# Regrouping the second batch's normalisation and reordering four projection units in an attention kernel

## The chip, the cores and the metric

The kernel runs on one core of a Trainium2 chip. The metric is device time in microseconds (us) of one execution, 2652.79 in the median of three runs before the change. Five engines work side by side and meet at semaphores: TensorE (PE) multiplies, VectorE (DVE), ScalarE (ACT) and GpSimd (POOL) work on elements, and SyncE (SP) issues the transfers, all of which go through one queue in the order of issue.

## The reference

Two batches of 2048 tokens with 1024 features go through one block: x is normalised over its features, projected to q, k and v of 16 heads, attended causally, projected again, normalised and added to x; a gated expert layer follows, which the change doesn't touch.

```python
q = (x @ wq.T + bq).reshape(B, S, H, hd)      # k and v likewise, x normalised
scores = jnp.einsum('bqhd,bkhd->bhqk', q, k) * inv_sqrt_hd
scores = jnp.where(causal[None, None, :, :], -jnp.inf, scores)
probs = jax.nn.softmax(scores, axis=-1)
attn = jnp.einsum('bhqk,bkhd->bqhd', probs, v).reshape(B, S, D)
return attn @ wo.T + bo
```

## The kernel before

**Pairs and steps.** Two heads of one batch make a pair; there are 16 pairs, 0 to 7 for batch 0 and 8 to 15 for batch 1. A pair has 24 steps. Three steps make a round: one long row tile of queries in two chunks of keys (8 blocks of 128 keys, then 8 down to 1), and one short row tile (1 up to 8 blocks). Each engine runs its own list of instructions, written out step by step in a function `body(p, kind)`, and waits for the others through counters.

**What a step holds.** In step i of pair p TensorE makes the scores of step i + 3 (`scores`, line 371), then a part of a projection unit for pair p + 1, then multiplies the probabilities of step i with v (`times_v`, lines 395 to 397). For step i + 3, VectorE takes the row maximum of both heads (`row_max`, 511), ScalarE the exponential (686) and the high half (692), GpSimd the low half (784), and SyncE transposes the result (`transpose_probs`, 278) into a ring of four tiles, `pt`. For each transpose SyncE waits until TensorE has used the tile that stood there four heads ago; so the transposes for step i + 3 follow TensorE's step i + 1. In every third step VectorE also evacuates the outputs of the last round (532 to 550). TensorE's scores of a step wait for the exponential of the first head of the step before it.

**Projection units.** q, k and v of a pair come in four chunks of 512 tokens each, twelve units, two steps for each unit. Their order is written out in `UNITS`: "mid" for most pairs, "pre" in pair 6 and "turn" in pair 7, the last two being the same list. The weights of a pair are fetched into one raw buffer, `w_raw` (line 269), and split into two halves by ScalarE (668) and VectorE (487). `SPLITS` puts the split of q at step 1, and those of k and v at the step after the last unit of k and of v. SyncE fetches the next weights one step after a split, behind that step's transposes, and only when VectorE has finished with `w_raw`. The order of the fetches is k, v, q.

**The second batch.** The normalised tokens lie in `arena`. Those of batch 0 must stay until pair 7 is projected, which pair 6 does. So batch 1's 16 tiles of tokens are normalised on the side during pairs 0 to 6, each in three parts: `norm_stats` (load waited for, 462, and GpSimd's `norm_scale`), `norm_apply` (472, and ScalarE's `xn_high`, 661), and `xn_low` (477). A tile is then stored to `xn_scratch` (301) and the next loaded into `x_in`, both ahead of SyncE's transposes of the following step. The parts stand at `FREE_STEPS`, the steps 1, 4, 7 and so on to 22 of each pair, three steps apart. From step 8 of pair 6 to step 14 of pair 7 SyncE transposes the tiles from `xn_scratch` into `arena` (line 263), one at each second step, in the order of chunks 0, 1, 3, 2.

Of the kernel before, what the change touches and what calls it, by code (L numbers as in the profile page):

```python
# [50 lines left out]
for i in range(QT // 2):  # L51
# [13 lines left out]
UNITS = {"start": [(m, c) for c in range(4) for m in "kqv"],  # L65
         "mid": [("k", 0), ("k", 1), ("k", 2), ("k", 3), ("q", 3), ("q", 0), ("v", 0), ("v", 1), ("v", 2), ("v", 3),
                 ("q", 1), ("q", 2)],
         "turn": [("k", 0), ("q", 0), ("v", 0), ("k", 1), ("q", 1), ("v", 1), ("k", 3), ("q", 3), ("k", 2), ("v", 3),
                  ("v", 2), ("q", 2)],
         "last": []}  # L70
UNITS["pre"] = UNITS["turn"]
# [10 lines left out]

LN_TILES = S // P


FREE_STEPS = [(p, i) for p in range(PAIRS) for i in range(1, NSTEP, PER_ROUND)][1:]
NORM_STEPS = {tile: FREE_STEPS[3 * tile:3 * tile + 3] for tile in range(LN_TILES)}


def norm_tiles(p, i, part):  # L90
    return [tile for tile, at in NORM_STEPS.items() if at[part] == (p, i)]

TURN_CHUNKS = [0, 1, 3, 2]
TURN_TILES = [4 * c + i for c in TURN_CHUNKS for i in range(4)]
# [12 lines left out]
def attend_phase(nc, x, w_pairs, unit_in, mask_in, xn_scratch, o_scratch, arena, fin):  # L109
    with ExitStack() as ctx:  # L110
# [120 lines left out]
        def next_split(p, kind, i):  # L231

            m = SPLITS[kind].get(i)
            target = p + 1 if m == "q" else p + 2
            return (target, m) if m and target < PAIRS else None
# [20 lines left out]
        def _(sp):  # L256
            def load_x(tile, sem_, b, t):
                sp.dma_start(tile[:], x_view[b, t]).then_inc(sem_, 16)
# [32 lines left out]
            def body(p, kind):  # L291
                for i in range(NSTEP):
                    n = TURN_STEPS.get(kind, {}).get(i)
                    if n is not None:
                        tile = TURN_TILES[n]
                        sp.wait_ge(xn_stored, 16 * (tile + 1))
                        sp.wait_ge(unit_done, units_before(HALF_PAIRS - 1, [(m, tile // 4) for m in "qkv"]))
                        transpose_x(LN_TILES + n, tile, xn_scratch[tile])
                    for tile in norm_tiles(p, i - 1, 2):
                        sp.wait_ge(xn_lo_done, LN_TILES + tile + 1)  # L300
                        sp.dma_start(xn_scratch[tile], xn[:]).then_inc(xn_stored, 16)
                        if tile + 1 < LN_TILES:
                            load_x(x_in, x_loaded[P_RING], 1, tile + 1)
                    if p == 0 and i == 0:
                        load_x(x_in, x_loaded[P_RING], 1, 0)
                    step = step_of(p, i, kind)
                    if step:
                        transpose_probs(*step)
                    split = next_split(p, kind, i - 1)
                    if split:  # L310
                        target, m = split
                        after = {"q": (target + 1, "k"), "k": (target, "v"), "v": (target, "q")}[m]
                        if after[0] < PAIRS:
                            load_weight(*after)
                    if i == 14:
                        store_rows(p, 0)
                    if p > 0 and i == 2:
                        store_rows(p - 1, 1)
                    if kind == "last" and i == 0:
                        sp.wait_ge(unit_done, N_UNIT * PAIRS)  # L320
                        sp.wait_ge(s_done, NTASK * (PAIRS - 1))
                        sp.wait_ge(mix_set, 2)
                        for k in range(4):
                            sp.dma_start(wo_raw[k], fin["w_view"][k]).then_inc(wo_loaded[k], 16)
                        for tile, source in fin["loads"]:
                            sp.dma_start(tile, source).then_inc(fin_loaded, 16)
                    if kind == "last" and i >= 4 and i < KT:
                        sp.wait_ge(wo_lo_done, i - 3)
                        sp.dma_start(wo_raw[i % 4], fin["w_view"][i]).then_inc(wo_loaded[i % 4], 16)
                if kind == "last":  # L330
                    store_rows(p, 1)
# [120 lines left out]
        def _(dve):  # L452
# [141 lines left out]
            def body(p, kind):  # L594
                for i in range(NSTEP):
# [13 lines left out]
                        split_weight(*split)  # L609
                    if i % PER_ROUND == 0:  # L610
                        row_min(p, i // PER_ROUND)
                    for tile in norm_tiles(p, i, 0):
                        norm_stats(LN_TILES + tile, x_in, x_loaded[P_RING], tile)
                    for tile in norm_tiles(p, i, 1):
                        norm_apply(LN_TILES + tile, x_in)
                    for tile in norm_tiles(p, i, 2):
                        xn_low(LN_TILES + tile, x_in, xn)
                    if kind == "last":
                        if i == 0:
                            dve.wait_ge(unit_done, N_UNIT * PAIRS)  # L620
# [37 lines left out]
        def _(act):  # L658
# [59 lines left out]
            def body(p, kind):  # L718
                for i in range(NSTEP):
# [16 lines left out]
                        rows_high(2 * p + (0 if i == 13 else -1))  # L736
                    if kind == "last" and 2 <= i < 2 + KT:
                        wo_high(i - 2)
                    for tile in norm_tiles(p, i, 1):
                        if tile > 0:  # L740
                            act.wait_ge(xn_stored, 16 * tile)
                        xn_high(LN_TILES + tile, x_in, xn)
                if kind == "last":
                    rows_high(2 * p + 1)

# [23 lines left out]
        def _(pool):  # L769
# [39 lines left out]
            def body(p, kind):  # L809
                for i in range(NSTEP):  # L810
# [11 lines left out]
                        long_rows(*((p, i // PER_ROUND - 1) if i else (p - 1, N_ROUND - 1)))  # L822
                    if i == 13 or i == 1 and p > 0:
                        rows_low(2 * p + (0 if i == 13 else -1))
                    for tile in norm_tiles(p, i, 0):
                        norm_scale(LN_TILES + tile)
                if kind == "last":
                    long_rows(p, N_ROUND - 1)
                    rows_low(2 * p + 1)
# [608 lines left out]
```

## Time and profile before

| | us |
|---|---|
| runs | 2650.32, 2658.9, 2652.79 |
| median | 2652.79 |
| the profiled execution | 2650.32 |
| its span, first to last instruction | 2648.1 |
| TensorE busy | 2362.3 (89%) |
| GpSimd busy | 1813.9 (68%) |
| VectorE busy | 1752.9 (66%) |
| ScalarE busy | 1696.3 (64%) |

The span lies 2.2 us inside the execution's own time. The attention loop runs from about 150 to 2162 us; the rest is the first batch's preparation before it and the output projection with the expert layer behind it. A granted clock of 1.00 is TensorE's full 2.4 GHz.

### The profile page before, as it was taken

What the parts mean: (1) busy time and instruction counts of PE and PEld (TensorE: products, weight loads), DVE (VectorE), ACT (ScalarE), POOL (GpSimd) and SP (SyncE); (2) the same over time, 40 slices, a digit from 0 to 9 for tenths busy, and PEclk for the clock granted to TensorE, in tenths of its full rate; (3) what the DMA queues carried; (4) which work ended last, traced back from release to release, by engine and by line L of the source; (5) the groups of instructions that cost most, each with busy time, mean ns of one, the idle gap of its engine ahead of it and who ended that gap; (6) DMA issues with size and microseconds to landing.
All of it is one profiled execution on the core that took longest, in us unless ns stands there. A gap on an engine that the chain in (4) does not pass through costs nothing. (4 is left out here: it accounts for less than half of the span.)

```text
span 2648.1 us, 73681 instructions
## 1 busy us (share of the span) xinstructions
PE 2362.3 (89%) x29650; PEld 1508.7 (57%) x29650; DVE 1752.9 (66%) x3751; ACT 1696.3 (64%) x2425; POOL 1813.9 (68%) x1543
## 2 busy tenths in 40 slices
PE   3789999999999997899999999999997549999995
PEld 2457576666656655556675757676674325444543
DVE  6466767666766654566656666666656836888887
ACT  2277778777777765667777777777776533444444
POOL 2278788878878775778778778887887533555453
PEclk9999999999999998999999999999998669999997
DMA  8499999999999999999999999999999875777773
GB/s 200 102 165 192 193 191 204 181 188 182 199 180 186 183 179 183 187 175 177 175 164 178 169 174 168 184 164 173 171 167 190 162 142 111 155 156 152 148 157 95
DMA packets 1433793, 450.33 MB, mean 170 GB/s; under 512 B 1410256, under 2 KB 1411680, under 8 KB 1433456
## 3 DMA queue, kind: packets, MB, share of 16 engines
q1 hardware_dynamic: 1433456, 445.63, 92.9%
q8 instruction: 236, 3.87, 0.6%
q14 instruction: 101, 0.83, 0.1%
HBM read 68.01 MB, written 41.94 MB: 42 GB/s over the span
## 5 line engine op out<-in xcount | busy, mean ns | idle before, releaser
L784 POOL TENSOR_TENSOR hl<-probs,hl 128x1024 f16<-128x1024 f32 (+7 forms) x768 | 1227.7, 1609 | 449.9 <-ACT hl L692 447.4
L511 DVE TENSOR_REDUCE neg_max<-s_ps 128x1 f32<-128x1024 f32 (+7 forms) x768 | 696.3, 907 | 408.5 <-PE s_ps L377 342.7
L686 ACT ACTIVATE probs<-s_ps,exp_bias 128x1024 f32<-128x1024 f32 (+7 forms) x768 | 655.0, 853 | 475.7 <-DVE exp_bias L514 471.2
L692 ACT ACTIVATE hl<-probs 128x1024 f16<-128x1024 f32 (+7 forms) x768 | 620.5, 808 | 46.3 <-DMA pt<-hl 22.2
L395 PE MATMUL o_ps<-v,pt 128*128 128x65 f16 x4352 | 456.2, 195 | 88.4 <-DMA pt<-hl 71.1
L371 PE MATMUL s_ps<-nat 64*128 64x512 f16 (+3 forms) x3840 | 439.3, 358 | 70.6 <-ACT probs L686 68.7
L395 PEld LDWEIGHTS o_ps<-v,pt 128*128 128x128 f16 x4352 | 406.3, 98 | 136.1 <-DMA pt<-hl 65.6
L396 PE MATMUL o_ps<-v,pt 128*128 128x65 f16 x4352 | 456.1, 196 | 0.0
L397 PE MATMUL o_ps<-v,pt 128*128 128x65 f16 x4352 | 454.2, 194 | 0.0
L424 PE MATMUL u_ps<-arena,w 128*128 128x512 f16 x992 | 384.8, 388 | 55.2 <-DMA arena<-hl 41.2
L396 PEld LDWEIGHTS o_ps<-v,pt 128*128 128x128 f16 x4352 | 406.1, 98 | 27.1 <-issue 0.3
L397 PEld LDWEIGHTS o_ps<-v,pt 128*128 128x128 f16 x4352 | 406.7, 99 | 0.0
L425 PE MATMUL u_ps<-arena,w 128*128 128x512 f16 x992 | 381.5, 385 | 0.0
L426 PE MATMUL u_ps<-arena,w 128*128 128x512 f16 x992 | 381.0, 384 | 0.0
L420 PE MATMUL u_ps<-w,arena 128*128 128x128 f16 x1984 | 340.7, 220 | 1.8 <-DVE full L503 1.8
L421 PE MATMUL u_ps<-w,arena 128*128 128x128 f16 x1984 | 339.4, 220 | 0.0
L422 PE MATMUL u_ps<-w,arena 128*128 128x128 f16 x1984 | 339.3, 220 | 0.0
L371 PEld LDWEIGHTS s_ps<-nat 64*128 64x128 f16 x3840 | 162.5, 96 | 219.0 <-issue 91.2
L420 PEld LDWEIGHTS u_ps<-w,arena 128*128 128x128 f16 x1984 | 194.1, 98 | 28.8 <-issue 20.9
L424 PEld LDWEIGHTS u_ps<-arena,w 128*128 128x128 f16 x992 | 97.5, 98 | 197.4 <-issue 85.2
L1054 PE MATMUL proj_ps<-arena,ot 128*128 128x512 f16 x512 | 196.2, 383 | 14.1 <-DMA ot<-o_scratch 14.1
L1055 PE MATMUL proj_ps<-arena,ot 128*128 128x512 f16 x512 | 195.9, 383 | 0.0
(147 smaller groups left out, 3774.2 us busy)
## 6 DMA issues: line engine op xcount, KB each, us to landing
w_raw<-in_w_pairs SPq DMA_DIRECT2D x48, 576.0 KB, 4.8
o_scratch<-o_hl SPq DMA_DIRECT2D x128, 128.0 KB, 3.5
x_in_c<-in_x SPq DMA_DIRECT2D x32, 512.0 KB, 5.9
out<-result SPq DMA_DIRECT2D x32, 512.0 KB, 4.2
pt<-hl SPq DMA_TRANSPOSE x768, 4.5
probs<-in_x SPq DMA_DIRECT2D x16, 512.0 KB, 4.7
x_in<-in_x SPq DMA_DIRECT2D x16, 512.0 KB, 5.3
xn_scratch<-xn SPq DMA_DIRECT2D x16, 512.0 KB, 3.8
```

The costliest lines, as they stand in the source:

```text
L371: mm = nc.tensor.matmul(s_ps[(n + h) % S_RING][:, at:end], qk[HEADS[h], q, rows], qk[HEADS[h], k, keys], start=(q == q_lo), stop=(q == q_h ...
L395: nc.tensor.matmul(dst, lo, v_hi, start=(first and k == 0), stop=False)
L396: nc.tensor.matmul(dst, hi, v_lo, start=False, stop=False)
L397: mm = nc.tensor.matmul(dst, hi, v_hi, start=False, stop=(last and k == nb - 1))
L420: nc.tensor.matmul(dst, xt[:, 1, k, toks], hi[:, k, :], start=first, stop=False)
L424: nc.tensor.matmul(bank, lo[:, k, :], xt[:, 0, k, toks], start=first, stop=False)
L425: nc.tensor.matmul(bank, hi[:, k, :], xt[:, 1, k, toks], start=False, stop=False)
L426: mm = nc.tensor.matmul(bank, hi[:, k, :], xt[:, 0, k, toks], start=False, stop=last)
L511: nc.vector.tensor_reduce(neg_max[:, r, acc, h:h + 1], s_ps[n % S_RING][:, 0:nb * P], AX_X, ALU.max, negate=True).then_inc(max_done, 1)
L686: nc.scalar.activation(probs[n % P_RING][:, 0:nb * P], s_ps[n % S_RING][:, 0:nb * P], ACT.Exp, bias=exp_bias[:, r, acc, h:h + 1], scale=SO ...
L692: nc.scalar.activation(hl[n % HL_RING][:, 0:nb * P], probs[n % P_RING][:, 0:nb * P], ACT.Copy).then_inc(p_hi_done, 1)
L784: nc.gpsimd.tensor_tensor(hl[n % HL_RING][:, w:2 * w], probs[n % P_RING][:, 0:w], hi, ALU.subtract).then_inc(p_lo_done, 1)
```

## The change

The three parts of a tile's normalisation stand on three steps in a row, beginning at steps 5, 12 and 19 of pairs 0 to 4 and at step 5 of pair 5, which holds the sixteenth tile. SyncE loads a tile three steps before the first part, and stores it in the step of the third part; both stand behind that step's transposes. The transposes from `xn_scratch` wait for all sixteen stores in place of their own. In the list "turn" (and "pre") units seven to ten become q3, k3, v3, k2 in place of k3, q3, k2, v3.

```diff
-         "turn": [("k", 0), ("q", 0), ("v", 0), ("k", 1), ("q", 1), ("v", 1), ("k", 3), ("q", 3), ("k", 2), ("v", 3),
+         "turn": [("k", 0), ("q", 0), ("v", 0), ("k", 1), ("q", 1), ("v", 1), ("q", 3), ("k", 3), ("v", 3), ("k", 2),
                   ("v", 2), ("q", 2)],
...
-FREE_STEPS = [(p, i) for p in range(PAIRS) for i in range(1, NSTEP, PER_ROUND)][1:]
-NORM_STEPS = {tile: FREE_STEPS[3 * tile:3 * tile + 3] for tile in range(LN_TILES)}
...
+NORM_STEPS = [{3 * p + i: 5 + 7 * i for i in range(3)} for p in range(5)] + [{15: 5}] + [{}] * (PAIRS - 6)
...
-                        sp.wait_ge(xn_stored, 16 * (tile + 1))
+                        sp.wait_ge(xn_stored, 16 * LN_TILES)
...
-                    for tile in norm_tiles(p, i - 1, 2):
-                        sp.wait_ge(xn_lo_done, LN_TILES + tile + 1)
-                        sp.dma_start(xn_scratch[tile], xn[:]).then_inc(xn_stored, 16)
-                        if tile + 1 < LN_TILES:
-                            load_x(x_in, x_loaded[P_RING], 1, tile + 1)
-                    if p == 0 and i == 0:
-                        load_x(x_in, x_loaded[P_RING], 1, 0)
                     step = step_of(p, i, kind)
                     if step:
                         transpose_probs(*step)
+                    for tile, at in NORM_STEPS[p].items():
+                        if i == at - 3:
+                            if tile >= 1:
+                                sp.wait_ge(xn_lo_done, LN_TILES + tile)
+                            load_x(x_in, x_loaded[P_RING], 1, tile)
+                        if i == at + 2:
+                            sp.wait_ge(xn_lo_done, LN_TILES + tile + 1)
+                            sp.dma_start(xn_scratch[tile], xn[:]).then_inc(xn_stored, 16)
...
-                    for tile in norm_tiles(p, i, 0):
-                        norm_stats(LN_TILES + tile, x_in, x_loaded[P_RING], tile)
-                    for tile in norm_tiles(p, i, 1):
-                        norm_apply(LN_TILES + tile, x_in)
-                    for tile in norm_tiles(p, i, 2):
-                        xn_low(LN_TILES + tile, x_in, xn)
+                    for tile, at in NORM_STEPS[p].items():
+                        if i == at:
+                            norm_stats(LN_TILES + tile, x_in, x_loaded[P_RING], tile)
+                        if i == at + 1:
+                            norm_apply(LN_TILES + tile, x_in)
+                        if i == at + 2:
+                            xn_low(LN_TILES + tile, x_in, xn)
```

ScalarE's `xn_high` moves to step `at + 1` and GpSimd's `norm_scale` to step `at` in the same way.

## Rows read from the trace of the kernel before

**Rows 1.** Busy time by stretch: length, busy us (instructions), granted clock, DMA share, GB/s.

```profile
263.00:890.20 627.20, 593.76 (x8481) 398.52 (x8480) 434.27 (x876) 466.12 (x656) 508.84 (x379) 0.99 1.07 189
890.20:1169.60 279.40, 247.36 (x3392) 161.60 (x3392) 147.73 (x324) 182.61 (x260) 191.88 (x141) 0.95 1.03 181
1169.60:1776.80 607.20, 587.34 (x8483) 395.33 (x8484) 380.49 (x812) 454.47 (x649) 483.04 (x351) 1.00 1.02 173
```

**Rows 2.** Timeline, VectorE's first instruction after pairs 6 and 12: start, us, instruction, wait.

```profile
1026.44 0.43 DVE L532 TENSOR_TENSOR o_part<-o_ps,factor 128x260 f32<-128x260 f32 x1 [1.46 <-PE o_ps L397]
...
1776.87 0.43 DVE L532 TENSOR_TENSOR o_part<-o_ps,factor 128x260 f32<-128x260 f32 x1 [0.70 <-PE o_ps L397]
```

**Rows 3.** TensorE's waits, 150 to 890 us: total, times, longest.

```profile
PE o_ps L395 <- DMA pt<-hl: 23.1, 24, 3.7
PE s_ps L371 <- ACT probs L686: 10.6, 14, 1.4
```

**Rows 4.** Timeline of TensorE at the turn, pair 6 and pair 7.

```profile
905.31 0.61 PE L424 MATMUL u_ps<-arena,w 128*128 128x512 f16 x1 [2.65 <-DVE w L487]
...
1046.65 0.61 PE L424 MATMUL u_ps<-arena,w 128*128 128x512 f16 x1 [7.00 <-DVE w L487]
...
1129.60 0.58 PE L424 MATMUL u_ps<-arena,w 128*128 128x512 f16 x1 [3.86 <-DMA arena<-xn_scratch]
```

**Rows 5.** Busy time by stretch, after two of these waits.

```profile
1046.60:1052.00 5.40, 5.35 (x17) 2.05 (x18) 0.00 (x0) 2.06 (x5) 4.48 (x4) 0.50 0.86 169
1129.60:1136.00 6.40, 6.40 (x42) 2.83 (x44) 0.00 (x0) 0.00 (x0) 1.30 (x2) 0.67 0.91 177
```

**Rows 6.** Timeline of SyncE's issues at the end of pair 6.

```profile
1013.33 0.57 SPq L269 DMA_DIRECT2D w_raw<-in_w_pairs  x1
...
1017.94 9.62 SPq L278 DMA_TRANSPOSE pt<-hl  x4
...
1038.89 0.57 SPq L269 DMA_DIRECT2D w_raw<-in_w_pairs  x1
```

**Rows 7.** Timeline of ScalarE in the same stretch.

```profile
1020.67 1.04 ACT L668 ACTIVATE w<-w_raw 128x1024 f16<-128x1024 f32 x1
...
1021.99 0.35 ACT L686 ACTIVATE probs<-s_ps,exp_bias 128x128 f32<-128x128 f32 x1
...
1044.21 1.06 ACT L668 ACTIVATE w<-w_raw 128x1024 f16<-128x1024 f32 x1 [4.85 <-DMA w_raw<-in_w_pairs]
```

**Rows 8.** The page's DMA issues: count, KB each, median us from issue to landing.

```profile
w_raw<-in_w_pairs SPq DMA_DIRECT2D x48, 576.0 KB, 4.8
```

**Rows 9.** Timeline at the end of pair 7, SyncE (to 1170 us) and TensorE.

```profile
1159.81 10.85 SPq L278 DMA_TRANSPOSE pt<-hl  x4
...
1170.04 1.47 PE L371 MATMUL s_ps<-nat 64*128 64x512 f16 x12 [0.42 <-ACT probs L686]
```

**Rows 10.** The tile x_in: durations ns min/median/max, first and last start; waits.

```profile
L472 DVE TENSOR_SCALAR x_in<-x_in,moments_a,rstd_a x16: 805/1288/2671, 182.5 to 885.5; 128x1024 f32<-128x1024 f32 x16
...
L477 DVE SCALAR_TENSOR_TENSOR xn<-x_in,xn x16: 1214/1548/2629, 196.9 to 901.2; 128x1024 f16<-128x1024 f32 x16
...
  DMA x_in<-in_x: 25.1, 14
```

**Rows 11.** Timeline of TensorE: step 6 of pairs 3 and 10, step 23 of pair 10.

```profile
548.60 0.24 PE L395 MATMUL o_ps<-v,pt 128*128 128x65 f16 x1 [3.74 <-DMA pt<-hl]
...
1449.12 0.20 PE L395 MATMUL o_ps<-v,pt 128*128 128x65 f16 x1 [1.46 <-DMA pt<-hl]
...
1530.72 0.34 PE L371 MATMUL s_ps<-nat 64*128 64x128 f16 x6 [1.40 <-ACT probs L686]
```

**Rows 12.** Timeline of VectorE, step 21 of pair 10.

```profile
1524.86 3.18 DVE L487 SCALAR_TENSOR_TENSOR w<-w_raw,w 128x1024 f16<-128x1024 f32 x1
```

**Rows 13.** Timeline of SyncE's issues, step 2 of pair 3.

```profile
530.20 0.77 SPq L301 DMA_DIRECT2D xn_scratch<-xn  x1
531.02 0.42 SPq L258 DMA_DIRECT2D x_in<-in_x  x1
```

More of the change, by code:

```diff
@@ L83 @@
 LN_TILES = S // P
-FREE_STEPS = [(p, i) for p in range(PAIRS) for i in range(1, NSTEP, PER_ROUND)][1:]
-NORM_STEPS = {tile: FREE_STEPS[3 * tile:3 * tile + 3] for tile in range(LN_TILES)}
-def norm_tiles(p, i, part):
-    return [tile for tile, at in NORM_STEPS.items() if at[part] == (p, i)]
+NORM_STEPS = [{3 * p + i: 5 + 7 * i for i in range(3)} for p in range(5)] + [{15: 5}] + [{}] * (PAIRS - 6)
 TURN_CHUNKS = [0, 1, 3, 2]
@@ L738, in body @@
                         wo_high(i - 2)
[L739 to L742, printed above, removed]
+                    for tile, at in NORM_STEPS[p].items():
+                        if i == at + 1:
+                            if tile > 0:
+                                act.wait_ge(xn_stored, 16 * tile)
+                            xn_high(LN_TILES + tile, x_in, xn)
                 if kind == "last":
@@ L824, in body @@
                         rows_low(2 * p + (0 if i == 13 else -1))
-                    for tile in norm_tiles(p, i, 0):
-                        norm_scale(LN_TILES + tile)
+                    for tile, at in NORM_STEPS[p].items():
+                        if i == at:
+                            norm_scale(LN_TILES + tile)
                 if kind == "last":
```

## The prediction

> **What bounds the kernel now.** First the busy table by stretch: the attention loop runs its 16 head pairs at a nearly even pace, and in pairs 8 to 12 (1169.6 to 1776.8 us) TensorE is busy 587.3 of 607.2 us at the full clock [rows 1]. TensorE is the bound there; every other engine has room. So a microsecond of other work costs nothing until it keeps TensorE waiting. The five pairs 1 to 5, which do the same attention work and carry most of the second batch's normalisation besides, take 627.2 us [rows 1]; their ends are read from VectorE's first instruction of the next pair [rows 2]. Normalisation therefore costs 20.0 us in five pairs, or 4.0 us a pair. Pairs 6 and 7, where the second batch's tokens replace the first's, take 279.4 us where two of the quiet pairs take 2 x 607.2 / 5 = 242.9 [rows 1]: 36.5 us too many. The change touches both places and nothing else, so at most some 56 us stand to be moved.
>
> Next the waits of TensorE. In the normalising stretch the longest in total are for transposed probabilities (23.1 us) and for ScalarE's exponentials (10.6) [rows 3]. At the turn, three single waits matter: 2.65 us and 7.00 us for the weights of q, and 3.86 us for the last token tiles [rows 4]. A wait costs more than itself, because the clock falls: after the wait that ends at 1046.65 TensorE works from 1046.6 to 1052.0 at a granted clock of 0.50, that is 1.2 GHz, so 5.4 us ran at half speed and 2.7 us were lost on top of the 7.00 [rows 4, 5].
>
> **The order of the units.** In pair 7 the old order asks for token chunk 2 with its ninth unit, at step 16, two steps after the last tile of it was sent for; the new order asks with the tenth, at step 18. The 3.86 us wait goes [rows 4], and with it its low clock: the 6.4 us of work behind it have a mean grant of 0.67, so 6.4 x 0.33 = 2.1 us were lost [rows 5]. Gain: 5.9 us, to rounding. One step of cover (5 us) would have been enough; two are given.
>
> The same edit has a second effect, which the list doesn't show. The last k unit moves from ninth to tenth, so the split of k's weights moves from step 18 to 20, while the last v unit stays eleventh and its split at 22. There is one raw buffer for the three weights: SyncE may fetch v's only after k's split, so the fetch moves from its step 19 to its step 21, and ScalarE wants it at 22. SyncE issues it behind the two transposes of step i + 3, and these wait for TensorE to have used the tiles of step i + 1; SyncE is thus two or three steps behind. Before, the fetch left at 1013.33 and ScalarE used it at 1020.67 without a wait [rows 6, 7]. Two steps later in the same queue is the point after the four transposes that end at 1017.94 + 9.62 = 1027.56 [rows 6]. A fetch takes about 4.7 us to land (4.8 in the median of all 48; the one issued at 1038.89 let ScalarE go at 1044.21, 5.3 us on) [rows 6, 7, 8]. So ScalarE stands from 1020.7 to 1032.3, then splits (1.04). Queued behind it is the exponential that before ran at 1021.99, and for that one waits TensorE's first scores of pair 7, at 1026.4 [rows 2, 7]. It comes at 1032.3 + 1.0 + 0.4 + about 0.2 for the hand-over = 1033.9. TensorE waits 7.4 us, and 2.7 of clock as after the other 7 us wait: 10.1.
>
> Part comes back. The present 7.00 us wait for q has the same pattern (fetch behind late transposes), and with TensorE held up, SyncE's backlog is gone. I let it shrink to the 2.65 us of pair 6, which gives 4.4 and some 1.0 of clock: 5.4. Net in pair 6 and early pair 7: +4.7.
>
> At the end of pair 7 the same: the four transposes that begin at 1159.81 end at 1170.66, landing 1175.3, exponential through at 1176.8; TensorE wanted it at 1170.04 - 0.42 = 1169.6 [rows 9]. 7.2 us, less the 0.42 already waited there, plus 2.7: +9.5. No wait for q follows there, since the next pair wants q only with its fifth unit. Off this I take 3 us over both turns, an estimate, for transposes that catch up while TensorE stands. Turn: 4.7 + 9.5 - 5.9 - 3.0 = +5.3. Bounds: if each fetch lands as TensorE asks, -5.9; if nothing is given back and nothing caught up, 10.1 + 9.5 - 5.9 = +13.7.
>
> The Trainium skill (DMA: Bandwidth & Descriptors, Specifications, and Latency and other measured facts) gives 358 GB/s from HBM and about 2 us of fixed cost. As an estimate, that makes 3.6 us for a fetch of 576 KB, and with it the two waits would be 1.1 us shorter each, the turn +3.1. The landings of this trace, 1 us longer, speak against it.
>
> **The normalisation.** The sixteen tiles keep all their instructions. Before, the three parts of a tile lie three steps apart, always on a step without the evacuation of outputs; now they lie on three steps in a row, from steps 5, 12 and 19, so that one part always meets the evacuation, and SyncE loads three steps ahead and stores two steps after. The distance from a load to its use stays as it was: before, a load stood ahead of the transposes of step i and was used at i + 2; now it stands behind those of at - 3 and is used at `at`. So VectorE's waits for x_in, 25.1 us over 14 of the tiles, remain [rows 10]. For each of pairs 0 to 4:
> - SyncE's step 2 already has four stores of outputs, and TensorE waited 1.46 us at step 6 of pair 10 [rows 11]. Now a load stands before them: 0.43 us to issue, and 512 KB, which at the stretch's 189 GB/s is 2.8 us of the queue [rows 1]. 0.4 to 3.2; I take 0.8, since part meets slack.
> - Step 14 likewise with a store of xn. 0 to 3.2; I take 0.8.
> - Step 21 is VectorE's fullest: evacuation, two maxima of 1024, a unit, and v's split, which takes 3.18 us and ends at 1528.04; TensorE then waits 1.40 us, until 1530.72, for the exponential behind the next maximum [rows 11, 12]. xn's low part, 1.2 to 2.6 us [rows 10], now stands ahead of that maximum. +1.6 (0 where the split is short, up to 2.6).
> - The rest (x_in late, rstd waited for, the applying step on the evacuating step 6): 0.5 a tile, 1.5 (0 to 3).
> - The low clock behind the longer of these waits: 0.7 (0 to 1.7 each in two places).
>
> That is 5.4 a pair, 27 in five pairs, and 1 for the sixteenth tile, 28, against 19.6 now (the 20.0, less 0.4 by which pair 0 is quick and pair 6's part counts). +8. Its ends: small items alone, 1.0 a pair, is 5 + 1 - 19.6 = -14; all items high, about 9 a pair, is +26.
>
> The Trainium skill (SBUF — State Buffer, SBUF: two separate sides) says that VectorE and GpSimd lock one port pair for a whole instruction, the later one waiting. The applying instruction, 0.81 us alone and up to 2.67 here, fits [rows 10]. By that rule alone its cost is the same at whatever step it stands, which is for the first rival below.
>
> **Sum.** 2650.3 (the profiled execution; span 2648.1) + 5.3 + 8.0 = 2663.6. The three runs have their median 2.5 us above that execution; I put the forecast between, at 2665.
>
> **The rivals.**
> - Normalisation costs what it did, turn as worked out: 2655.6. For it: mean instruction times don't depend on the step, and VectorE has 30% idle time [rows 1]. 0.24.
> - Faster: today's cost is SyncE's store and load side by side ahead of the transposes (0.77 and 0.42 us, followed by a 3.74 us wait of TensorE [rows 11, 13]); apart, each stays within SyncE's slack, a pair costs 1.0 us, and -13.6 + 5.3 gives 2642.0. It decides from 1.1 us a pair down. Against: both now fall beside the output stores. 0.15.
> - VectorE falls behind over its three steps in a row, the wait at step 23 grows to over 3 us in every pair and the clock falls each time: 9 a pair, 2682. 0.13.
> - The fetch of v is hidden after all, or lands just in time (turn -5.9), normalisation +8: 2652. Against: it is queued behind the very transposes timed above. 0.06.
> - The forecast itself: 0.42.
>
> **Numbers.** Within 0.3% (8 us) is what a measurement of this kernel can't tell from no change: the first and fourth rival, 0.30. Faster is the second, 0.15. Slower is the forecast and the third, 0.55. The range leaves out half of the second's case and half of the third's, so 2642 to 2682; with both signs in it, the forecast's own is 2658 to 2674.
>
> **What would show it.** Right: TensorE's waits for ScalarE's exponentials of some 7 us at the starts of pairs 7 and 8, ScalarE standing there for w_raw; no wait for xn_scratch; the 7 us wait for q's weights under 3; waits at steps 6, 18 and 23 of pairs 0 to 4 longer, pairs 1 to 5 over 630 us. Wrong: pairs 1 to 5 below 620 us, or v's fetch landed before ScalarE asks.

## The result, and the profile after

| | before | after |
|---|---|---|
| median, us (five runs each) | 2653.22 | 2678.71 |
| range, us | 2650.32 to 2658.9 | 2669.97 to 2682.93 |
| the profiled execution | 2650.32 | 2673.91 |
| its span | 2648.1 | 2671.7 |

The changed kernel is slower: its time is 1.0095 of the time before, with a 95% interval of 1.0077 to 1.0113. The forecast had 2665 us: the direction is right and the time falls within the range, but the loss is 25.5 us by the medians and 23.6 by the profiled executions, where the forecast's sum had 13.3. The time lies outside the forecast's own 2658 to 2674.

First, where the time went. The busy table by stretch, cut at the same places as [rows 1] (columns as there):

```profile
269.30:912.00 642.70, 601.60 (x8483) 400.64 (x8484) 427.39 (x875) 465.48 (x657) 501.17 (x377) 0.98 1.03 183
912.00:1186.00 274.00, 242.49 (x3393) 159.95 (x3392) 144.98 (x322) 180.50 (x253) 191.80 (x141) 0.96 1.03 180
1186.00:1800.70 614.70, 588.31 (x8484) 394.71 (x8484) 379.00 (x812) 455.83 (x651) 483.20 (x351) 0.99 1.01 172
```

Pairs 1 to 5 take 642.7 us, 15.5 more than in [rows 1]; pairs 6 and 7 take 5.4 less, and pairs 8 to 12 take 7.5 more, since one new wait stands just behind the cut, in step 0 of pair 8. Pair 0 and the preparation account for another 6.3 (pair 1 begins at 269.3, not 263.0). Normalisation is thus the large item: the end of pair 5 comes at 912.0 and not 890.2, 21.8 us late, out of 23.6. The turn is the small one: +4.0 us over pairs 6 to 8, from 912.0 to 1316.8 (404.8) against 890.2 to 1291.0 (400.8). What follows is 2.2 us shorter.

The waits of TensorE in the normalising stretch, over the 150 to 890 us of [rows 3] (total us, times, longest; up to the end of pair 5 at 912.0 the exponentials' total is 11.7):

```profile
PE o_ps L388 <- DMA pt<-hl: 31.2, 19, 4.0
PE s_ps L364 <- ACT probs L680: 10.3, 12, 2.4
PE o_ps L388 <- issue: 3.7, 4, 2.1
```

Waits for the transposed probabilities, which hang on SyncE's queue, grew from 23.1 to 31.2 us. Those for exponentials nearly kept their total, but the longest is 2.4 us instead of 1.4. TensorE's timeline has it in step 23 of pair 2, and waits for transposes in steps 6 and 13 of pair 3, the first of which answers to the 3.74 us of [rows 11]:

```profile
522.64 0.51 PE L364 MATMUL s_ps<-nat 64*128 64x128 f16 x6 [2.44 <-ACT probs L680]
...
567.33 0.24 PE L388 MATMUL o_ps<-v,pt 128*128 128x65 f16 x1 [3.76 <-DMA pt<-hl]
...
603.39 0.20 PE L388 MATMUL o_ps<-v,pt 128*128 128x65 f16 x1 [0.78 <-DMA pt<-hl]
```

The turn, in the same view. The first and the third row answer to the first two of [rows 4], the last to TensorE's of [rows 9]:

```profile
927.22 0.39 PE L417 MATMUL u_ps<-arena,w 128*128 128x512 f16 x1 [3.62 <-DVE w L480]
...
1048.65 0.61 PE L364 MATMUL s_ps<-nat 64*128 64x512 f16 x2 [7.94 <-ACT probs L680]
...
1065.33 0.61 PE L417 MATMUL u_ps<-arena,w 128*128 128x512 f16 x1 [3.63 <-DVE w L480]
...
1159.33 0.23 PE L388 MATMUL o_ps<-v,pt 128*128 128x65 f16 x1 [3.24 <-DMA pt<-hl]
...
1193.60 1.01 PE L364 MATMUL s_ps<-nat 64*128 64x512 f16 x3 [7.56 <-ACT probs L680]
```

The waits of 7.94 and 7.56 us at the starts of pairs 7 and 8 are the forecast's late fetches of v. The wait of 7.00 us for q's weights is 3.63. The 3.86 us wait for xn_scratch is gone; two steps later stands one of 3.24 us for a transpose, which the forecast did not have. The timelines of SyncE and of ScalarE show the reason of the wait of 7.94 us:

```profile
1041.99 1.23 SPq L261 DMA_DIRECT2D w_raw<-in_w_pairs  x1
```

```profile
1046.83 1.06 ACT L662 ACTIVATE w<-w_raw 128x1024 f16<-128x1024 f32 x1 [9.19 <-DMA w_raw<-in_w_pairs]
1048.16 0.35 ACT L680 ACTIVATE probs<-s_ps,exp_bias 128x128 f32<-128x128 f32 x1
```

The fetch is issued at 1041.99. ScalarE stands 9.19 us for it, splits the weights, and only then does the exponential that TensorE wants; at 1048.65 TensorE resumes. Before, the same fetch left 13.1 us ahead of the end of pair 6 [rows 2, 6]; now it leaves 1.3 us behind it (pair 6 ends at 1040.7). The changed wait for all sixteen stores to `xn_scratch` plays no part: the last of them is issued at 841.7 us and the first transpose from there at 964.3.

**The excess table.** Two kernels that differ in order can't be compared by one wait. For the comparisons below I took the length of every step (the end of the last product with v of a step, less that of the step before) and subtracted the shortest length that the profiles show for a step of that number, in whatever pair (most pairs have the list "mid"). What remains is that step's excess. Its zero is thus a convention; only differences between rows are read. "6-7" and so on are steps of pairs 0 to 5, added up; (7,0) is step 0 of pair 7. One execution each, us:

```
       end of    pairs 0-5                           pairs 6-8
       pair 5    total   6-7    13   18-19   23      total  (7,0) (8,0) (7,2) (7,16) (7,18-19)
before  890.2     47.7  12.2   0.2    7.6   6.0       50.9    0.8   0.5   9.7    5.9    0.0
after   912.0     68.5  25.2   4.7   11.7  14.4       54.9    9.4   9.9   5.3    0.0    6.3
e8      910.7     67.4  23.4   4.9   12.8  14.3       57.5    9.7   9.0   5.4    0.0    3.8
e1      891.1     49.2  13.3   0.4    7.2   6.3       61.7   10.3  10.0   5.4    0.0    5.6
e2      911.9     69.7  25.1   4.8   16.0  13.2       50.1    0.8   0.7   7.6    5.8    0.0
e3      895.0     51.8  15.7   0.8    7.2   6.0       63.4   10.6  10.0   5.4    6.0    0.0
e4      906.6     63.7  31.0   4.9   13.7   1.5       60.2   11.0   9.8   5.2    0.0    4.7
e5      893.2     51.7  13.2   6.1    1.3   3.6       59.2   10.8   9.0   5.1    0.0    2.9
e9      895.2     53.3  23.4   4.3    1.0   5.6       63.1   10.9  10.3   5.1    0.0    6.1
e10     899.1     56.2  14.2   0.0   11.1  20.5       56.7    9.7   9.3   5.4    0.0    3.2
e6      894.5     51.9   8.5   1.6    8.0   5.7       53.5    0.0   0.7   6.1    0.0    3.6
e7      901.2     57.5  13.0   2.4    4.5   9.4       53.0    0.9   0.7   5.2    6.4    0.0
e11     884.4     42.6   1.1   0.4    1.0   2.9       52.9    0.8   0.2   7.8    6.6    0.0
e12     892.9     49.4  10.6   5.4    0.0   5.1       52.7    9.4  10.2   5.3    0.0    0.9
e13     879.7     37.7   0.6   1.0    0.1   8.8       51.2    0.1   0.6   4.4    0.0    0.9
e14     883.4     40.6   2.1   0.0    0.9   9.4       55.8    1.0   0.6   4.3    6.2    0.0
```

Its grain: e8 is the changed kernel once more, and e1, e3, e6 and e7 have the normalisation of before. Their pairs 0 to 5 lie 1.5, 4.1, 4.2 and 9.8 us above the first profile of before. So differences under about 4 us in one total say nothing, one of 10 can come from a single execution, and the first profile of before was a quick one: the mean of the five is 51.6.

### The profile page after: what moved, and what is told of

Same layout as the page of the kernel before. It is cut to its first block and busy times, and to the rows that moved or that the text cites. A ratio compares the mean times of both kernels' runs of the same rounds, so it can differ in the third digit from the quotient of the medians.

```text
span 2671.7 us, 73681 instructions
## 1 busy us (share of the span) xinstructions
PE 2364.8 (89%) x29650; PEld 1506.2 (56%) x29650; DVE 1747.5 (65%) x3751; ACT 1696.2 (63%) x2425; POOL 1808.3 (68%) x1543
```

## The experiments

### Which half costs: the order, the regrouping, the split (e1 to e3)

`e1_units_only` is the kernel before with only the new list of units:

```diff
- ("v", 1), ("k", 3), ("q", 3), ("k", 2), ("v", 3),
+ ("v", 1), ("q", 3), ("k", 3), ("v", 3), ("k", 2),
```

> The kernel before with the new order of the units alone. Theory A (as the changed kernel's trace reads): TensorE waits some 7.9 us for an exponential at the start of pair 7 and some 7.6 us at the start of pair 8, each with about 2.7 us of low clock behind it; the 3.86 us wait for the last token tiles is gone and the 7.0 us wait for q's weights shrinks to 3.6. Sum +4 us, 2654 in the profiled execution, ratio 1.001 to 1.003. Theory B (the two new waits carry the whole slowdown and the regrouping is harmless): +20 us or more, ratio from 1.007.

`e2_regroup_only` is the changed kernel with that line set back.

> The changed kernel with the old order of the units. Theory A: the regrouped normalisation costs 20 us more than the old one in pairs 0 to 5, and the turn reads as before (waits 7.0 and 3.9 us): ratio 1.006 to 1.009, about 2672. Theory B (regrouping harmless): ratio within 1.002 of 1.

`e3_k_split_late` keeps the old order and moves only the split of k's weights to step 20:

```diff
+SPLITS["pre"] = SPLITS["turn"] = {1: "q", 20: "k", 22: "v"}
```

> The kernel before with its old order of units, but the split of k's weights in pairs 6 and 7 moved from step 18 to step 20, and nothing else. It isolates the fetch. Theory A (v's fetch is late because it waits for k's split): the two waits of 7 to 8 us at the starts of pairs 7 and 8 appear without the new order; the 3.86 us wait stays; the q wait shrinks. +10 us (8 to 13), ratio 1.003 to 1.005. Theory B (the new waits come from the order of the units itself, e.g. k2 needed sooner than it is ready): no such waits, ratio 1.000.

Each ratio here and below is to runs of the kernel before on the same chip, whose median is given. Against 2661.48: e1 2670.14, ratio 1.0039 (1.0023 to 1.0056); e2 2674.43, 1.0057 (1.0040 to 1.0074); e3 2676.58, 1.0055 (1.0035 to 1.0076). Both halves cost, and their ratios multiply to 1.0096, that of the whole change. e1 and e3 cost more than their expectations allowed (1.003 and 1.005 at most), e2 a shade less (1.006 at least). In the excess table e1 has the turn's new waits and none of the normalisation's, e2 the reverse: the halves are independent. e3 shows the cause of the turn's: with the old order and its wait at step 16, one changed split step brings both late fetches and 12.5 us over pairs 6 to 8, in TensorE's timeline:

```profile
1036.11 2.75 PE L372 MATMUL s_ps<-nat 64*128 64x512 f16 x12 [8.07 <-ACT probs L687]
...
1183.53 2.74 PE L372 MATMUL s_ps<-nat 64*128 64x512 f16 x12 [7.73 <-ACT probs L687]
```

### What in the regrouping costs (e4, e5, e9)

`e4_low_late` moves only the last part of each pair's third tile, `xn_low` and its store, from step 21 to 22:

```diff
+low_at = lambda at: at + 3 if at == 19 else at + 2
...
-                        if i == at + 2:
+                        if i == low_at(at):
```

> The changed kernel with the low part (and the store) of the third tile of each pair moved from step 21 to step 22, behind the row maximum for which TensorE waits at step 23. Theory A (the low part stands ahead of that maximum): TensorE's waits at step 23 of pairs 0, 2 and 4 fall from 2.2 to 2.4 us to 1.4 or less, the clock behind them stays full, and pairs 0 to 5 lose about 8 us: 2666 in the profiled execution against 2674. Theory B (step 23 waits because of VectorE's whole load in three steps, not the order): step 23 unchanged.

`e5_io_apart` moves two of SyncE's transfers out of the steps that hold the output stores: the load of the first tile from step 2 to 1, the store of the second from step 14 to 15.

```diff
-                        if i == at - 3:
+                        if i == (1 if at == 5 else at - 3):
...
-                        if i == at + 2:
+                        if i == (15 if at == 12 else at + 2):
```

> The changed kernel with only SyncE's places changed: the load of the first tile at step 1 in place of 2, the store of the second at step 15 in place of 14, so that neither is issued in the step of the output stores. Theory A (they delay the transposes that queue behind the output stores): the waits at step 6 of pairs 1 to 5 fall by 1.5 to 2 us each and those at 18 by about 1, with their low clock; 12 us less in pairs 0 to 5, 2662. Theory B (what counts is the extra traffic and issue anywhere in the queue): the waits move a step with them, and pairs 0 to 5 change by less than 3 us.

Against 2659.16: e4 2676.68, ratio 1.0075 (1.0062 to 1.0087); e5 2669.60, 1.0033 (1.0016 to 1.0050). e4 removed its wait (step 23: 14.4 to 1.5 us), yet pairs 0 to 5 fell only 4.8, where about 8 were expected: steps 6 and 7 rose from 25.2 to 31.0. Whether that is the gain given back or a difference between executions, one profile can't tell, and the time's interval overlaps that of the changed kernel. e5 took 16.8 us off pairs 0 to 5 (68.5 to 51.7): 12.0 at steps 6 and 7, 10.4 at 18 and 19, 10.8 at 23, and 14.3 came back at steps 1, 2 and 20. TensorE's waits over pairs 0 to 5 in e5:

```profile
PE o_ps L388 <- DMA pt<-hl: 30.4, 28, 3.3
PE s_ps L364 <- ACT probs L680: 5.1, 6, 2.4
```

The total is as large as after the change, but in 28 pieces, the longest 3.3 us. Step 23 shows something more. VectorE's low part of a third tile takes 3.08 us or 1.21, and in these two kernels TensorE waits more than 0.4 us behind it only where it takes 3.08. VectorE in pair 4, after and then in e5:

```profile
775.00 3.09 DVE L470 SCALAR_TENSOR_TENSOR xn<-x_in,xn 128x1024 f16<-128x1024 f32 x1
```

```profile
759.88 1.21 DVE L470 SCALAR_TENSOR_TENSOR xn<-x_in,xn 128x1024 f16<-128x1024 f32 x1
```

TensorE's wait behind these, in the same order:

```profile
780.71 0.34 PE L364 MATMUL s_ps<-nat 64*128 64x128 f16 x6 [2.22 <-ACT probs L680]
```

```profile
763.71 0.34 PE L364 MATMUL s_ps<-nat 64*128 64x128 f16 x6 [0.29 <-ACT probs L680]
```

After the change, the third tile's low part is the long one in pairs 0, 2 and 4, whose step 23 has 4.0 to 4.2 us of excess each; in e5 it is long in pair 2 alone, which has 2.5 of e5's 3.6. So e5's gain at step 23 is a shift of VectorE against its neighbours, brought about by the moved transfers but not asked for.

`e9_low_io` has both edits.

> The changed kernel with both repairs of the regrouping: the third low part and its store one step later, and SyncE's load and store out of the steps of the output stores. Theory A (both act, each on its own waits): pairs 0 to 5 some 20 us shorter than in the changed kernel, near the kernel before; ratio 1.002 to 1.004, what is left being the turn's 8 us. Theory B (the two share a cause): no better than the moved transfers alone, 17 us.

Against 2653.12: 2665.52, 1.0040 (1.0027 to 1.0054), pairs 0 to 5 at 53.3. The two repairs don't add up. With SyncE's transfers apart, moving the low part brought nothing more.

### Issue time or traffic (e10), and the changed kernel again (e8)

`e10_load_small` is the changed kernel with 15 of the 16 loads cut to an eighth. SyncE issues the same instructions; the second batch is computed from other data.

```diff
-                            load_x(x_in, x_loaded[P_RING], 1, tile)
+                            if tile == 0:
+                                load_x(x_in, x_loaded[P_RING], 1, tile)
+                            else:
+                                sp.dma_start(x_in[:, 0:P], x_view[1, tile][:, 0:P]).then_inc(x_loaded[P_RING], 16)
```

> The changed kernel with the loads of the second batch's tiles 1 to 15 cut to 128 of 1024 columns (so the second batch is computed from other data; all instructions stay). It tells the 512 KB of a load from its place in SyncE's list. Theory A (traffic): the waits at step 6 fall from some 3 us to 1.5 in the mean, those at step 13 go, 10 us less. Theory B (SyncE's issue time of 0.5 to 1 us a transfer): both stay within 0.5 us.

> The changed kernel once more, beside the others of this set: how well its waits repeat. Pairs 0 to 5 within 4 us of the first profile, the waits at the starts of pairs 7 and 8 again 7.5 to 8 us, ratio 1.007 to 1.010.

e10: 2665.25, 1.0051 (1.0034 to 1.0069); e8: 2685.15, 1.0107 (1.0081 to 1.0134). With small loads steps 6 and 7 fall from 25.2 to 14.2 and step 13 from 4.7 to 0.0, both the steps that a load stands ahead of (steps 2 and 9). So it is the 512 KB in the queue that delay the transposes behind them, not the 0.4 to 1.1 us that a load takes to issue. Steps 18 and 19, behind a store, stay (11.7 to 11.1), as they should. Step 23 rose to 20.5, with waits for exponentials up to 4.5 us:

```profile
PE o_ps L391 <- DMA pt<-hl: 20.8, 13, 3.7
PE s_ps L367 <- ACT probs L683: 19.1, 16, 4.5
```

The low part of the third tile is the long one in four pairs here (1 to 4), where it was in three. The longest wait, though, stands in pair 0, whose low part took 1.34 us: there the two VectorE instructions of v's split ahead of it are the long ones, 2.04 and 3.16 us where the changed kernel's pair 0 has 0.22 and 1.22. VectorE and TensorE in e10:

```profile
256.51 3.16 DVE L483 SCALAR_TENSOR_TENSOR w<-w_raw,w 128x1024 f16<-128x1024 f32 x1
```

```profile
263.62 0.34 PE L367 MATMUL s_ps<-nat 64*128 64x128 f16 x6 [4.48 <-ACT probs L683]
```

So what moves step 23 here is how long VectorE's instructions in step 21 take, the low part or the split; none of these waits is for a transfer.

### The output stores (e11, e12)

In both kernels SyncE issues four output stores one after another in step 2 and again in step 14. `e11_stores_spread` is the kernel before with one in each of steps 2 to 5 and 14 to 17:

```diff
-                    if i == 14:
-                        store_rows(p, 0)
-                    if p > 0 and i == 2:
-                        store_rows(p - 1, 1)
+                    if 14 <= i < 18:
+                        store_rows(p, 0, [i - 14])
+                    if p > 0 and 2 <= i < 6:
+                        store_rows(p - 1, 1, [i - 2])
...
```

`store_rows` now takes the numbers of the stores that it is to issue.

> The kernel before with the four output stores of steps 2 and 14 issued one in each of steps 2 to 5 and 14 to 17. If TensorE's waits at steps 6 and 18, which also pairs without normalisation show, come from SyncE issuing four stores (2.6 to 2.9 us) ahead of the transposes, they fall to under 0.5 us in all pairs but the last: 2 us and 1 us with their low clock, 16 times, 20 to 40 us less, ratio 0.985 to 0.993, faster than both kernels. If they come from the traffic alone they spread and the ratio stays above 0.997.

`e12_spread_changed` is the same edit on the changed kernel.

> The changed kernel with the output stores spread over steps 2 to 5 and 14 to 17. Theory A (the regrouping costs what it does at steps 6 and 18 because its load and store meet the bunched output stores): the regrouping's extra 17 us over the old one shrink to under 8 in pairs 0 to 5, and this kernel is 30 us or more faster than the changed one, ratio 0.997 to 1.001 to the kernel before. Theory B (its transfers are late anywhere, the two costs add): 20 us faster than the changed one, and 25 us slower than the spread stores in the kernel before, ratio 1.002.

e11: 2628.73, 0.9912 (0.9894 to 0.9931) of 2653.12. e12: 2641.89, 0.9956 (0.9934 to 0.9979) of 2655.90. TensorE's waits over pairs 0 to 5, of e11 and then of e12:

```profile
PE o_ps L395 <- DMA pt<-hl: 24.0, 30, 1.7
PE s_ps L371 <- ACT probs L686: 9.4, 13, 1.5
```

```profile
PE o_ps L388 <- DMA pt<-hl: 33.3, 31, 3.2
PE s_ps L364 <- ACT probs L680: 4.9, 4, 1.9
```

In e11 the total of the waits for transposes is as large as before, but the longest is 1.7 us and not 3.7. Steps 6 and 7 fall from 12.2 to 1.1. Only 5.8 of the profile's 18.7 us come before the end of pair 5, and 13.3 in pairs 9 to 14 (724.5 us, then 711.2), which hold no normalisation: the bunched stores cost there too. What regrouping adds in pairs 0 to 5, 20.8 us with the stores bunched (68.5 less 47.7), is 6.8 with them spread (49.4 less 42.6). By means over all profiles with the same normalisation steps and the same stores it is 16.9 (68.5 less 51.6) and 9.1 (49.4 less 40.3, of e11, e13 and e14). So by the two ways of counting a little under a half or two thirds of its cost is the meeting with the bunched stores. The rest stays behind the loads: steps 6 and 7 are 9.5 us longer in e12 than in e11, step 13 is 5.0. Steps 1 and 20 are 11.8 longer, which no run explains, and other steps give most of all this back.

### Where step 16's gain goes (e6, e7, e13, e14)

In `e6_spare_new` every second weight from v of pair 8 on goes into a second raw buffer (x_in, by then unused, made wider); the fetch runs two weights ahead, so no split waits for it. It stands on the kernel before with the new list; `e7_spare_old` is the same with the old one.

```diff
+        def raw_of(at):
+            if at >= SPARE and (at - SPARE) % 2 == 0:
+                return x_wide, w_loaded2, (at - SPARE) // 2 + 1
+            return w_raw, w_loaded, at if at < SPARE else SPARE - 1 + (at - SPARE + 1) // 2
...
-                    sp.wait_ge(w_lo_done, weight_at(p, m) - 1)
+                    sp.wait_ge(w_lo_done, at - (1 if at < SPARE else 2))
```

> The kernel before with the new order of units, and from v of pair 8 on every second weight fetched into the idle x_in buffer (512 bytes a partition wider), so that a fetch no longer waits for the split just before it. Theory A (the fetch behind the last split is the whole of the two 7.5 us waits and of the q wait): no wait for exponentials above 2 us at the starts of pairs 7 and 8, q's wait at step 2 of pair 7 falls from 7.0 (before) and 3.6 (new order) to 2.7. Against the new order alone 15 to 20 us less, against the kernel before -5 to -9, ratio 0.997 to 0.998, if the 3.86 us saved at step 16 are not given back at step 18. Theory B: they are given back there (3.1 us wait for transposed probabilities, as in the new order alone), then -2 to -5.

> The same spare buffer with the old order of units. It tells the order's own worth once the fetch is out of the way. Theory A (the new order saves 5.9 us): this is 5 to 6 us slower than the spare buffer with the new order, with a 3.9 us wait at step 16 of pair 7. Theory B (the saving is given back at step 18): the two are within 2 us in pairs 6 to 8.

Against 2659.16: e6 2663.34, 1.0028 (1.0011 to 1.0046); e7 2661.73, 1.0018 (1.0003 to 1.0033). Neither is faster than the kernel before, where e6 was expected at 0.997 to 0.998. The spare buffer takes both late fetches away from the new order: (7,0) and (8,0) are 0.0 and 0.7, 19.6 us less than in e1. But pairs 6 to 8 are only 8.2 us shorter than in e1 (53.5 against 61.7). A part of the rest stands one step on, at (7,1), which the table doesn't show: its excess is 5.5 us in e6 and 0.0 in e1, with TensorE's wait for a transpose. TensorE in e6:

```profile
1044.40 0.19 PE L409 MATMUL o_ps<-v,pt 128*128 128x65 f16 x1 [3.02 <-DMA pt<-hl]
```

Between e6 and e7 the new order gains nothing. Both stretches of pairs 6 to 8, in the busy tables of e6 and of e7, are 403.5 and 403.0 us long. The 6.4 us at step 16 of e7 are in e6 3.6 at steps 18 and 19, 4.3 more at (7,1), and smaller items of both signs.

`e13_spread_spare_new` and `e14_spread_spare_old` are these two with the output stores spread as well.

> The kernel before with spread output stores, the spare weight buffer and the new order of units. Theory A (with SyncE in time, the 3.86 us saved at step 16 of pair 7 are no longer given back at step 18): 5 to 6 us less than with the old order, and q's wait falls from 6.2 to 2.6 us; pairs 6 to 8 about 12 us shorter than with spread stores alone: 2617, ratio 0.986. Theory B (given back wherever it stands): no better than spread stores alone but for q's wait, 2624.

> The same with the old order of units. Theory A: 5 to 6 us slower than with the new order, the 3.9 us wait for the last token tiles standing. Theory B: within 2 us of it.

Against 2655.90: e13 2623.77, 0.9875 (0.9847 to 0.9903); e14 2631.87, 0.9897 (0.9874 to 0.9919). The busy table over pairs 6 to 8, of e13 and then of e14:

```profile
879.70:1280.80 401.10, 364.09 (x5091) 241.53 (x5092) 228.31 (x487) 273.76 (x391) 290.75 (x212) 0.97 1.05 181
```

```profile
883.40:1289.20 405.80, 367.64 (x5092) 242.58 (x5092) 228.95 (x487) 273.83 (x391) 291.36 (x212) 0.96 1.04 179
```

With the stores of step 14 out of the way steps 18 and 19 cost 0.9 us, and the new order is worth 4.7 us here: the 6.2 of step 16 less small items. So what took the gain back at steps 18 and 19 was SyncE, still behind from the four stores of step 14, and not the order itself. The two intervals overlap (0.9847 to 0.9903, 0.9874 to 0.9919); that the order gains rests on this stretch of one profile each. The expectation that pairs 6 to 8 would be about 12 us shorter than with spread stores alone was missed: they are 1.7 shorter (51.2 against e11's 52.9), with 3.8 us of excess at (7,1). Most of e13's gain is e11's, and the intervals of these two overlap as well. By its median e13 is the best version: 1.25% under the kernel before and, by the two ratios (0.9875 / 1.0095 = 0.978), 2.2% under the changed one. It has the old normalisation steps, spread stores, the spare buffer and the new order.

## Why the prediction was right in direction and wrong in size

The step that failed is the price of the load that moved to step 2, 0.8 us a pair where 2.6 were measured, and beside it the load at step 9, which was not priced at all; both are in the part on the normalisation below.

**v's late fetch: right.** The forecast had waits of 7.4 and 7.2 us; they are 7.94 and 7.56, with 9.4 and 9.9 us of excess at (7,0) and (8,0), where it had 10.1 and 9.5. e3 makes them with the split alone, e6 takes them away with a buffer alone, though less than half of the time comes back with them.

**The wait for q: about right.** 7.00 us became 3.63 and not 2.65; "under 3" was missed. Its step, (7,2), gave back 4.4 us where 5.4 were forecast.

**Step 16: the step was right and its end was missed.** The 3.86 us wait and its clock are gone, as forecast, 5.9 us. But the prediction let that gain reach the end; 6.3 us came back at steps 18 and 19 (3.8 in e8, 5.6 in e1), except where the output stores were spread. The question of what is late next was put to the fetches and not to this gain. The 3.0 us taken off for transposes that catch up have a counterpart: the table's five columns at the turn add up to 14.0 us more than before and the total of pairs 6 to 8 to 4.0, so the other steps are 10.0 shorter; in e8, e1 and e3 they are 4.4, 3.6 and 2.6 shorter. The clearest of them is step 23 of pair 6, 4.5 us of excess before and 1.8 to 2.0 in these four; whether transposes that catch up are the cause no run shows. In sum the turn was forecast at +5.3. In the profiles of kernels with the new order, one raw buffer and bunched stores pairs 6 to 8 are 4.0, 6.6, 10.8, 9.3, 8.3, 12.2 and 5.8 us longer than before (after, e8, e1, e4, e5, e9, e10): 8.1 in the mean, within the given bounds of -5.9 and +13.7. That the first profile of after has 4.0, near the forecast, is in part luck.

**The normalisation: the failed step.** Forecast +8, measured +20.8 against the first profile of before and about +17 against the mean of those with unchanged normalisation. The upper end, "all items high, about 9 a pair", was added up wrongly: the bullets' own ends make 15.4 a pair, so it was no bound. By its bullets:
- Step 21, sized 1.6 a pair, 8 in five: step 23's excess rose by 8.4. Right in sum, but not as 1.6 in each pair: it is some 4 us, clock included, in the three pairs in which the low part takes 3.09 us, 0.4 in pairs 1 and 3, and 1.5 in pair 5, which has no third tile.
- Step 2's load, sized 0.8 a pair from a range of 0.4 to 3.2: steps 6 and 7 rose by 13.0, or 2.6 a pair. This is the failing term. "Part meets slack" was wrong: there was no slack, since four output stores are issued right behind the load, ahead of the transposes (SyncE's timeline, step 2 of pair 3, of after):

```profile
552.18 1.06 SPq L250 DMA_DIRECT2D x_in<-in_x  x1
553.30 0.42 SPq L261 DMA_DIRECT2D w_raw<-in_w_pairs  x1
553.76 2.91 SPq L280 DMA_DIRECT2D o_scratch<-o_hl  x4
556.78 14.18 SPq L270 DMA_TRANSPOSE pt<-hl  x6
```

  The end that the bullet worked out from the bytes of the load, 2.8 us, was the one to take; it was nearest to the row that it quoted beside it, the 3.74 us wait behind a store and a load [rows 11, 13].
- The load of step 9 was not priced at all; step 13 rose by 4.5, 0.9 a pair. This and the 1.8 us a pair missing at step 2 are 13.5 us in five pairs; the whole gap is 20.8 - 8 = 12.8.
- The load of step 16 was not priced either, and here nothing was lost: step 20, behind it, has 1.1 us of excess in six pairs, 2.2 before and 1.4 in e10, whose load there is an eighth. The same 512 KB thus cost 2.6, 0.9 or nothing by their place in the queue.
- Step 14's store, sized 0.8: steps 18 and 19 rose by 4.1, 0.8 a pair. Right.
- What went away was not seen. Steps 3, 4, 9, 14 and 15, where TensorE before stood for exponentials (up to 1.3 us at step 9) and transposes, fell from 12.6 us of excess to 1.8. The four rises above add up to 30.0; this and small changes elsewhere make it 20.8. Which of the moved parts had caused those waits no run tells.
- "VectorE's waits for x_in remain" was wrong, in the change's favour: 25.1 us over 14 tiles are 4.9 over 4. A load lands 4.6 us after its issue in the median (5.3 before), and VectorE is ready for the tile 5.2 us after the issue, not 3.4. The tile's rows, after:

```profile
L465 DVE TENSOR_SCALAR x_in<-x_in,moments_a,rstd_a x16: 803/806/1398, 179.1 to 822.2; 128x1024 f32<-128x1024 f32 x16
...
L470 DVE SCALAR_TENSOR_TENSOR xn<-x_in,xn x16: 1208/1923/3093, 183.5 to 832.8; 128x1024 f16<-128x1024 f32 x16
...
  POOL rstd_a L773: 9.1, 5
  DMA x_in<-in_x: 4.9, 4
```

  What it bought can't be told from the waits that went away at steps 3 to 15.

**The rivals.** That normalisation costs what it did fell with e2 (1.0040 to 1.0074). The faster one, store and load apart, fell too: they were parted from each other, but put beside four output stores, which cost more (e5 moves two of them off and the excess drops by 16.8 us). Its place, SyncE's queue, was where the change is decided, with the other sign. And VectorE's three steps in a row made no wait of over 3 us at step 23 in the changed kernel: 2.44 us was the longest, and three pairs of five have one of over 2.2. The fourth rival, v's fetch hidden after all, fell with the two waits of over 7 us. That rival's time, 2682, came nearer than the forecast's 2665, but its mechanism gave 8.4 us of the 20.8. With e10's 4.48 us one such wait exists in the record, in one pair.

**The applying instruction** was forecast to cost the same at any step by the rule of the Trainium skill (SBUF — State Buffer, SBUF: two separate sides): VectorE, where an instruction has two inputs in SBUF or runs in a mode with two ports, and GpSimd, where it reads SBUF, share one port pair and exclude each other for a whole instruction. Here its median fell from 1.29 to 0.81 us, and the low part's rose from 1.55 to 1.92, up to 3.09. The timelines of after show it in pair 2, VectorE first and then GpSimd:

```profile
516.94 3.09 DVE L470 SCALAR_TENSOR_TENSOR xn<-x_in,xn 128x1024 f16<-128x1024 f32 x1
```

```profile
516.77 5.24 POOL L779 TENSOR_TENSOR hl<-probs,hl 128x1024 f16<-128x1024 f32 x2 [1.29 <-ACT hl L686]
```

And in pair 3:

```profile
647.31 1.21 DVE L470 SCALAR_TENSOR_TENSOR xn<-x_in,xn 128x1024 f16<-128x1024 f32 x1
```

```profile
647.39 3.12 POOL L779 TENSOR_TENSOR hl<-probs,hl 128x1024 f16<-128x1024 f32 x1 [1.28 <-ACT hl L686]
```

Where GpSimd is first, VectorE takes 3.09 us; where VectorE is first, it takes 1.21 and GpSimd 3.12, which ends 1.99 us behind VectorE's. The trace is as the rule has it; what I read out of it, that the step makes no difference, does not hold, since the step decides which instruction meets a GpSimd one.

## What to carry to other kernels

Price a transfer that is moved in a queue by what is already queued at its new place: with four stores beside it, 512 KB more cost about the bytes' whole time, 2.6 us a pair, where a guess of "part meets slack" had 0.8; at two other steps the same bytes cost 0.9 and nothing. And add up the upper ends of the items before one of them is called a bound. When a wait is taken away, look for the next place that the same queue serves, a step or two on; the gain counts only if nothing there is late as well. And where one raw buffer is fetched just behind its last use, the step of that last use is a term of the schedule: moving it by two steps put 9.8 and 9.5 us on one step at each of two places (e3), 12.5 net over three pairs.

## What the runs showed of the hardware that was not expected

- A wait of TensorE well below the 7 us of [rows 4] already costs clock. TensorE was busy at a granted clock of 1.00 up to the 2.44 us wait that ends at 522.64; after it the busy table has a granted clock of 0.77 over 7.4 us, a mean between the two levels of 2.4 and 1.2 GHz, so 7.4 x 0.23 = 1.7 us were lost on top:

```profile
522.60:530.00 7.40, 7.36 (x82) 4.00 (x82) 2.42 (x9) 5.70 (x11) 6.33 (x6) 0.77 1.08 256
```

- The same total of waits costs less in small pieces. e11 kept 24.0 us of waits for transposes (30, none over 1.7), and the same matmuls kept TensorE busy 700.0 us from 150 us to the end of pair 5, at a granted clock of 1.00, against 704.1 at 0.99 before. Pairs 0 to 5 ended at 884.4, 879.7 and 883.4 in the three kernels with spread stores and the old normalisation, and at 890.2 or later in the five with bunched ones.
- Issuing a transpose was not slower behind the stores. Six took 14.18 us there, 2.4 each, and the four of [rows 6], with no store just ahead, 9.62, also 2.4 each. Over the whole kernel before one takes 1.17 us at the least, 1.87 in the median and 4.59 at the most. What bounds the longer ones (the queue, or the tiles that they wait for) no run tells apart.
- Single executions of kernels with the same instructions in pairs 0 to 5 differ by several us: pairs 0 to 5 with the old normalisation ended at 890.2, 891.1, 894.5, 895.0 and 901.2. What sets this stays open.
